# A two-layer recurrent block: unlooped projections, turned logits behind the next queries, three queues for a group's loads, wider gate rows

## What is computed

```python
x = L0_attn_x                                    # 2 x 2048 x 256, float32
xn = _layernorm(x)
s = _L0_attn_ref(xn, ...)                        # 16 heads of width 16, full attention, plus xn
g = _silu(_L0_ffn_ref(xn, ...))                  # 8 experts, two branches, gelu router, cumulative sums
x = x + s * g
xn = _layernorm(x)
s = _L1_attn_ref(xn, ...)                        # 16 heads, band |i - j| <= 64
g = _silu(_L1_ffn_ref(xn, ...))                  # below
x = x + s * g

def _L1_ffn_ref(x, weight, gate_w, lora_U, lora_V):
    gate = softmax(xt @ gate_w.T)                # 8 experts
    base = xt @ weight.T
    t = einsum('nh,erh->ner', xt, lora_U)        # 8 x 16 values per token
    lora = einsum('ne,eor,ner->no', gate, lora_V, t)
    return base + lora / 16
```

## Time and profile before

| | us |
|---|---|
| median of 3 runs | 2477.73 |
| lowest, highest | 2476.5, 2492.4 |
| profiled execution | 2464.94 |
| its span | 2463.20 |
| PE busy | 2211.5 (90% of the span) |
| DVE busy | 1840.1 (75%) |
| ScalarE busy | 1448.6 (59%) |
| POOL busy | 463.5 (19%) |
| mean granted PE clock | 0.952 |

### The profile page before, as it was taken

One profiled execution on the slowest core, in us unless ns is written; L12 is line 12 of the kernel. 1 busy time (PEld: TensorE's weight loads), 2 busy tenths in 40 slices (PEclk: granted clock), 3 DMA queues, 4 the chain that ended last, 5 costly groups with the idle time before them and its releaser, 6 DMA issues. The chain is left out here.

```text
span 2463.2 us, 44369 instructions
## 1 busy us (share of the span) xinstructions
PE 2211.5 (90%) x14912; PEld 1233.5 (50%) x14912; DVE 1840.1 (75%) x3240; ACT 1448.6 (59%) x2165; POOL 463.5 (19%) x673
## 2 busy tenths in 40 slices
PE   7786799999999999999999999988999986799988
PEld 5564333333333333333333333326888875566688
DVE  5553999999999999999999999913443565788846
ACT  4443177777777777777777777771222222266743
POOL 0000000000000000000000000003455510266745
PEclk8998599999999999999999999999999988589999
DMA  6766700310500500402205002006567469666564
GB/s 212 260 238 196 93 4 6 47 22 5 61 5 8 61 3 12 57 6 36 31 5 61 7 8 61 3 5 188 155 172 177 103 235 355 130 134 154 153 166 129
DMA packets 189121, 231.80 MB, mean 94 GB/s; under 512 B 72720, under 2 KB 122768, under 8 KB 186064
## 3 DMA queue, kind: packets, MB, share of 16 engines
q1 hardware_dynamic: 176048, 210.46, 35.0%
q10 hardware_dynamic: 7184, 14.10, 2.8%
q0 software_dynamic: 5728, 5.00, 0.9%
HBM read 138.97 MB, written 89.13 MB: 93 GB/s over the span
## 5 line engine op out<-in xcount | busy, mean ns | idle before, releaser
L1015 DVE TENSOR_REDUCE a_maxes<-a_ps_a 128x2 f32<-128x1024 f32 x1024 | 1202.3, 1221 | 112.0 <-PE a_ps_a L1136 108.3
L1080 ACT ACTIVATE a_prob<-a_ps_s 128x512 f32<-128x512 f32 (+1 forms) x1376 | 1035.8, 804 | 347.5 <-PE a_ps_s L1162 341.5
L1162 PE MATMUL a_ps_s<-a_Q,a_K 50*128 50x512 f32 x2048 | 593.8, 452 | 90.7 <-ACT a_prob L1080 90.4
L1136 PE MATMUL a_ps_a<-a_K,a_Q 48*128 48x512 f32 x2048 | 549.9, 454 | 25.6 <-DMA a_Q<-s_halves 14.2
L1174 PE MATMUL a_ps_o<-a_prob,a_V 128*17 128x512 f32 x4096 | 539.8, 599 | 0.1
L1162 PEld LDWEIGHTS a_ps_s<-a_Q,a_K 50*128 50x128 f32 x2048 | 277.4, 185 | 505.8 <-ACT a_prob L1080 456.6
L1136 PEld LDWEIGHTS a_ps_a<-a_K,a_Q 48*128 48x128 f32 x2048 | 244.9, 189 | 229.7 <-issue 107.9
L973 POOL DMA_DIRECT2D a_Q<-a_m_parts x128 | 64.5, 504 | 1285.3 <-DVE a_m_parts L1007 1278.6
L1626 ACT ACTIVATE a_prob<-a_ps_s 128x512 f32<-128x512 f32 (+1 forms) x256 | 135.7, 583 | 111.6 <-PE a_ps_s L1717 110.5
L1566 DVE CUSTOM_DVE_ANT_0 a_scratch<-a_ps_a,k_mask 128x256 f32<-128x256 f32 (+1 forms) x512 | 177.9, 411 | 30.0 <-PE a_ps_a L1681 28.0
L1681 PE MATMUL a_ps_a<-k_K,k_Q 48*128 48x256 f32 (+1 forms) x512 | 122.2, 363 | 32.5 <-PEq L89 21.7
(11 more groups left out here) (186 smaller groups left out, 2225.3 us busy)
## 6 DMA issues: line engine op xcount, KB each, us to landing
s_halves<-p_parts SPq DMA_DIRECT2D x64, 512.0 KB, 5.3
s_xT<-p_xT SPq DMA_DIRECT2D x64, 256.0 KB, 4.4
a_Q<-s_halves SPq DMA_DIRECT2D x186, 64.0 KB, 10.4
a_K<-s_halves SPq DMA_DIRECT2D x42, 256.0 KB, 9.6
s_v<-p_v_out SPq DMA_DIRECT2D x16, 544.0 KB, 4.5
s_cT<-p_cT SPq DMA_DIRECT2D x32, 256.0 KB, 3.6
k_wb<-s_w SPq DMA_DIRECT2D x16, 512.0 KB, 7.6
c_wb<-s_w SPq DMA_DIRECT2D x16, 512.0 KB, 7.2
```

What stands on the lines that cost most here:

```text
L1015: nc.vector.tensor_reduce(maxes[:, :, slot, qt, kc], ps_a[:, o:o + 2 * CH].rearrange("p (z k) -> p z k", z=2), AX.X, ALU.max).then_inc(a_d ...
L1080: nc.scalar.activation(prob[:, ring:ring + len(t), :].rearrange("p r q -> p (r q)"), ps_s[:, bank:bank + len(t) * CH], ACT.Exp, scale=scal ...
L1136: last = nc.tensor.matmul(ps_a[:, o + side * CH:o + (side + 1) * CH], Q[rows, q0:q0 + P], K[rows, k0:k0 + CH], start=True, stop=True)
L1162: last = nc.tensor.matmul(ps_s[:, bank + x * CH:bank + (x + 1) * CH], K[rows, k0:k0 + P], Q[rows, q0:q0 + CH], start=True, stop=True)
```

## The change

There are three parts.

1. `phase_project`: the three pairs of the loop are written out on all five engines, in both layers. In layer 0 the transposes of a chunk's logits (`turn_logits`) stand behind the next chunk's `queries_keys` on PE, and DVE's `logits` behind the next chunk's `rests(i, u, (2, 3))`. The last chunk's stand at the end.
2. Band: of the second group's loads SP keeps the keys of side 0 and has them ahead of `store_maxima(0)`; ScalarE keeps the keys of side 1, ahead of the ones; POOL gets all queries, under a semaphore of its own, for which PE waits too.
3. Last stage: `front` is one product with 392 columns (gate, U and weight together) into c_ps_x (4 banks), the attention projection goes to c_ps_s (2 banks), and c_ps_m keeps 2. `front`, `maximum` and `softmax` run three tiles ahead instead of two. `maximum` and `softmax` stand at the end of their engine's work for a tile. The wait of `front` on `wt_done` is gone; that on `out_read` stays, with OUTS = 4, and now stands ahead of the whole product.

The diff, cut to its core:

```diff
@@ -517,7 +517,7 @@
                         second_halves(sp, 0)
                     store_values(sp, i, u)
 
-            with sp.Fori(0, NCH - 1) as i:
+            for i in range(NCH - 1):
                 chunk_pair(i, True)
...
                     rests(i, u, (2, 3))
+                    if first and 2 * i + u > 0:
+                        logits(*divmod(2 * i + u - 1, 2))
...
                         row_statistics(nc, dve, L, i + 1, u, passed)
-                    if first:
-                        logits(i, u)
...
                 chunk_pair(i, True)
             chunk_pair(NCH - 1, False)
+            if first:
+                logits(NCH - 1, 1)
...
                 last.then_inc(log_ready, 1)
+
+            def turn_logits(c):
                 wait_apart(pe, logT_done, 2 * (c + 1), passed)
...
             def chunk_pair(i, more):
                 for u in range(2):
                     queries_keys(i, u)
+                    if first and 2 * i + u > 0:
+                        turn_logits(2 * i + u - 1)
                     if u == 0:
...
                 chunk_pair(i, True)
             chunk_pair(NCH - 1, False)
+            if first:
+                turn_logits(2 * NCH - 1)
...
-def load_next(eng, S, KQ, side, g, k):
-
-    done = KQ["loaded"][g % BAND_BUFS]
+def load_next(eng, S, KQ, side, g, k, done=None):
+
+    done = done or KQ["loaded"][g % BAND_BUFS]
...
-            return LOADS * (g // BUFS + 1) - (LOADS - EARLY_LOADS if g % BUFS == 0 else 0)
+            return LOADS * (g // BUFS + 1) - (LOADS - EARLY_LOADS, 2 * PARTS, 0)[g % BUFS]
...
+            for k in range(0, PARTS, 2):
+                load_next(sp, S, KQ, 0, 1, k)
             store_maxima(0)
-            for k in range(PARTS):
-                load_next(sp, S, KQ, 0, 1, k)
             load_v(sp, 0)
             load_v(sp, 1)
...
+            for k in range(1, PARTS, 2):
+                for side in range(2):
+                    load_next(pool, S, KQ, side, 1, k, pool_loaded)
             for s in range(STEPS):
                 mask(s)
...
+            for k in range(0, PARTS, 2):
+                load_next(act, S, KQ, 1, 1, k)
             for side in range(2):
                 for row in range(2):
                     r = side * SIDE + ROW_M0 + row
                     act.dma_start(f32(K[r:r + 1, :]), W["ones"][:, 0:BUFS * LONG // P]).then_inc(rows_set, DMA)
-            for k in range(PARTS):
-                load_next(act, S, KQ, 1, 1, k)
...
                         pe.wait_ge(kq_loaded[g % BUFS], loads_of(g) * DMA)
+                    if g == 1:
+                        pe.wait_ge(pool_loaded, 2 * PARTS * DMA)
...
         OUTS = 4
-        ps_gt = n_.ps("ps_gt", 2 * CH)
-        ps_out = n_.ps("ps_out", OUTS * CH)
+        ps_x = n_.ps("ps_x", OUTS * CH)
+        ps_s = n_.ps("ps_s", 2 * CH)
         ps_m = n_.ps("ps_m", 2 * CH)
...
             def front(i, j):
                 u, t = order[j]
                 n = TILES_BODY * i + j
-                gt, g = (j % 2) * CH, (j % OUTS) * CH
+                o = (j % OUTS) * CH
                 c = 2 * i + u
...
                 x = lambda s, k: xT[c % BUFS][:, s, k, t * P:(t + 1) * P]
-                pe.wait_ge(wt_done, n + 1)
-                split_matmul(nc, ps_gt[:, gt:gt + NGT], x, lambda s, k: W["gate"][:, s, k, 0:NGT], DK,
-                             True, True).then_inc(gt_ready, 1)
                 pe.wait_ge(out_read, n + 1)
-                split_matmul(nc, ps_out[:, g:g + D], x, lambda s, k: W["gate"][:, s, k, NGT:], DK,
-                             True, False)
+                split_matmul(nc, ps_x[:, o:o + NGT + D], x, lambda s, k: W["gate"][:, s, k, :], DK,
+                             True, False).then_inc(gt_ready, 1)
...
             def out(i, j):
                 n = TILES_BODY * i + j
-                g = (j % OUTS) * CH
+                g, o = (j % OUTS) * CH + NGT, (j % 2) * CH
+                pe.wait_ge(out_read, OUTS + n - 1)
                 pe.wait_ge(high, n + 1)
                 pe.wait_ge(low, 2 + n + 1)
 
-                split_matmul(nc, ps_out[:, g + D:g + 2 * D], lambda s, k: turned[:, j % 2, s, k * P:(k + 1) * P],
-                             lambda s, k: W["o1"][:, s, k, :], DK, False, True)
-                split_matmul(nc, ps_out[:, g:g + D], lambda s, k: turned[:, j % 2, s, D:D + P],
+                split_matmul(nc, ps_s[:, o:o + D], lambda s, k: turned[:, j % 2, s, k * P:(k + 1) * P],
+                             lambda s, k: W["o1"][:, s, k, :], DK, True, True)
+                split_matmul(nc, ps_x[:, g:g + D], lambda s, k: turned[:, j % 2, s, D:D + P],
                              lambda s, k: W["loraV"][:, s, 0, :], 1, False, True).then_inc(out_ready, 1)
...
             def body(i, more):
                 for j in range(TILES_BODY):
-                    if ahead(i, j, 2, more):
-                        front(*ahead(i, j, 2, more))
+                    if ahead(i, j, 3, more):
+                        front(*ahead(i, j, 3, more))
                     if ahead(i, j, 1, more):
                         turn(*ahead(i, j, 1, more))
                     out(i, j)
 
             front(0, 0)
             front(0, 1)
+            front(0, 2)
...
+                gt = (j % OUTS) * CH
+                act.wait_ge(top_done, n + 1)
+                if n > 1:
+                    act.wait_ge(soft, 2 * (n - 1))
+                nc.scalar.activation(ge[:, j % 2], ps_x[:, gt:gt + E1], ACT.Exp, bias=neg_top[:, j % 2:j % 2 + 1],
+                                     accum_out=total[:, j % 2:j % 2 + 1]).then_inc(ge_done, 1)
...
             def body(i, more):
                 for j in range(TILES_BODY):
-                    if ahead(i, j, 2, more):
-                        softmax(*ahead(i, j, 2, more))
                     if ahead(i, j, 1, more):
                         copies(*ahead(i, j, 1, more))
                     exponential(i, j)
+                    if ahead(i, j, 3, more):
+                        softmax(*ahead(i, j, 3, more))
...
+                gt = (j % OUTS) * CH
                 dve.wait_ge(gt_ready, n + 1)
-                nc.vector.tensor_reduce(neg_top[:], ps_gt[:, gt:gt + E1], AX.X, ALU.max, negate=True
-                                        ).then_inc(soft, 1)
+                if n > 1:
+                    dve.wait_ge(ge_done, n - 1)
+                nc.vector.tensor_reduce(neg_top[:, j % 2:j % 2 + 1], ps_x[:, gt:gt + E1], AX.X, ALU.max, negate=True
+                                        ).then_inc(top_done, 1)
...
             def body(i, more):
                 for j in range(TILES_BODY):
-                    two, one = ahead(i, j, 2, more), ahead(i, j, 1, more)
-                    if two:
-                        maximum(*two)
+                    three, two, one = (ahead(i, j, k, more) for k in (3, 2, 1))
                     if one:
                         rest(*one)
                     if two:
                         gates(*two)
-                    n, slot, g = TILES_BODY * i + j, j % 2, (j % OUTS) * CH
+                    n, slot, g = TILES_BODY * i + j, j % 2, (j % OUTS) * CH + NGT
                     gate_steps(nc, dve, n, sums[:, slot], W["bo"][:, 1], (x1_done, n + 1),
-                               gate[:, slot], eg[:, slot], ps_out[:, g + D:g + 2 * D],
-                               ps_out[:, g:g + D], exp_done, step, out_read, x1_done)
+                               gate[:, slot], eg[:, slot], ps_s[:, slot * CH:slot * CH + D],
+                               ps_x[:, g:g + D], exp_done, step, out_read, x1_done)
+                    if three:
+                        maximum(*three)
```

More of the change, by code:

```diff
@@ L532, in _ @@
         def _(pool):
-            with pool.Fori(0, NCH - 1) as i:
+            for i in range(NCH - 1):
                 for u in range(2):
@@ L617, in _ @@
             transposed(0, 0)
-            with dve.Fori(0, NCH - 1) as i:
+            for i in range(NCH - 1):
                 chunk_pair(i, True)
             chunk_pair(NCH - 1, False)
+            if first:
+                logits(NCH - 1, 1)
         @block.scalar
@@ L677, in _ @@
             turned(0, 0)
-            with act.Fori(0, NCH - 1) as i:
+            for i in range(NCH - 1):
                 chunk_pair(i, True)
@@ L755, in _ @@
             transposes(0, 0)
-            with pe.Fori(0, NCH - 1) as i:
+            for i in range(NCH - 1):
                 chunk_pair(i, True)
             chunk_pair(NCH - 1, False)
+            if first:
+                turn_logits(2 * NCH - 1)
 NG2 = NG // B
@@ L2155, in phase_combine_lora @@
         att = n_.sb("att", [P, BUFS, TT, D])
[L2156 to L2158 removed]
+        neg_top = n_.sb("neg_top", [P, 2])
+        ge = n_.sb("ge", [P, 2, E1])
+        total = n_.sb("total", [P, 2])
         inv = n_.sb("inv", [P, 1])
@@ L2291, in softmax @@
                 n = TILES_BODY * i + j
-                gt = (j % 2) * CH
-                act.wait_ge(soft, 3 * n + 1)
```

(8 more changed lines are left out.)

22 lines of the change are left out of this document (11 added, 11 removed).

## The result

| | us |
|---|---|
| before, median of 20 runs | 2476.39 |
| changed, median of 20 runs | 2492.31 |
| ratio, 95% interval | 1.0062, 1.0046 to 1.0078 |
| changed, profiled execution | 2485.8 (span 2484.2) |

The changed kernel is slower by 0.62%, some 15 us; the forecast was +11.1 (0.45%).

The account below looks back on a forecast made before the run. TensorE was taken to bound layer 0's projection, band and last stage, DMA layer 1's projection. Terms -22 + 0 - 5.5 + 38.6 = +11.1 on the 2477.73 median gave 2489 us; own range 2474 to 2502, 8 in 10 2466 to 2540.

Parts of the forecast that it names:

- Last stage, +38.6: Last stage: PE waits for DVE's gate before 28 fronts, tile 4.16 against 2.78 us, +38.6; bounds +33 to +45.
- The handoff: Last stage: 0.1 us from the gate's end at T + 2.77 to PE's six merged rows.
- the bound of 4.0 a tile: Last stage's lower bound: a tile period of 4.0 us with handoffs hidden, giving +33.
- Layer 0, -22: Layer 0's projection: moved logits -11.1, written-out loops -5.8 and clock -5, in sum -22; bounds -15 and -23.
- The logits' term of 11.1: Layer 0: seven of eight waits of 1.58 us before the turned logits go, -11.1.
- table loads and clock together (5.8 and 5): Layer 0, loops written out: five activation table loads go, -5.8; half-speed rows after their gaps go, -5 of 6.2.
- Layer 1, 0: Layer 1's projection: DMA engines are full, so gains wait at the stores of s_halves; 0, bounds -2 and +1.
- Band, -5.5: Band's start: second group's loads land at 2122.3, shortening PE's 8.04 us wait by 5.5; bounds 0 and 8.0.
- The clock did not fall in the last stage: First rival, last stage: pauses lower PE's clock, tile some 6.0 us, total 2540, or 2514 for half; chance 0.25.
- The second, that the wait does not bite: Second rival, last stage: DVE frees the banks before PE arrives; -37 in all, 2441; chance 0.07.
- If nothing else happened: Last stage: merged rows cost 0.30 us less than 1.37 per tile, so 32 tiles would give -9.6.
- The third rival: Projection and band: only moved logits pay, -11, and the band 0; total +28, 2505; chance 0.08.

Follow-up runs that it names:

- front behind out: The changed kernel with PE issuing front(j+3) after out(j) instead of ahead of turn(j+1): 2448.14 us, ratio 0.9875 to the kernel before.
- one gate step: front behind out, plus ScalarE's copies ahead of softmax (two tiles ahead) and c_weight dropped, its factor in the LoRA V weights: 2433.64 us, 0.9816 of before.

## Why the prediction was right

**Last stage, +38.6; measured +40.6 and +42.1.** This was the term that decides, and its mechanism held to the hundredth where it rests on rows of before: the gate ended at T + 2.77. Two small numbers were off. The handoff was 0.05, not 0.1. The six rows took 1.19 from start to start (2416.02 to 2417.21), not 1.07; without a wait ahead of them they take 1.07 (2392.36 to 2393.43 with front behind out) to 1.08 (2376.81 to 2377.89 with one gate step). So they cost 0.11 more after a pause, which unbroken rows can't show: in the stream the weight load of the first starts 0.11 ahead of its matmul (2376.70), behind the wait the two start together (2416.02). Tile 4.23 against 4.16. The 1.07 itself was partly luck: between 0.75 for 256 columns and 1.39 for 512 (1942.39 to 1943.78) interpolation gives 1.09, and 1.07 is 392/512 of 1.40. And the bound of 4.0 a tile gives +34, not +33. On the price of the rows the estimate by the Trainium skill, "TensorE: Matmul & The Clock Gate", section "Wait — 56ns, not 53.3ns?", was 0.995 for six; the traces have 1.07 to 1.08 in the stream.

**Layer 0, -22; measured -20.7, and -20.3 in the means.** The logits' term of 11.1 was measured as 12.8, table loads and clock together (5.8 and 5) as 7.1. The clock's share was put down to the table loads alone; that step was wrong. Of the four slow stretches that it counted in the kernel before, the two of h went with the table loads, and the two of queries stand behind the logits' wait. With the loops alone written out two stretches of slow queries were left, about 3 us, which is most of what is missing from the 10.8.

**Layer 1, 0; measured +1.6** over thirteen profiles, a little above my upper bound of 1. That whatever the engines gain waits at the stores fits what was measured, since the stage's own work kept its length; what the term lacks is the idle time between the last values and the band, 1.8 longer in the mean, and its cause stays open.

**Band, -5.5; measured -6.1 at the wait and -6.0 in the stage's mean.** The whole 8.04 went, and 1.9 came back at the maxima, which the prediction had named. But the 5.5 was worked out differently, as 8.04 less a wait of 2.55 for the queries; these landed at about 2105.4, 0.8 behind 2104.64, where PE came to stand, and the maxima at 2106.56 hid that. So the size is right in part by luck. POOL was faster at the issue than forecast, 6.1 us for twelve and not 10. By the Trainium skill, "DMA: Bandwidth & Descriptors", section "Issuing engines are not separate DMA queues", several issuers save only the time of the issue, which the prediction put at 3.4. The gain is more, since SP's loads had stood behind the wait for the maxima too, and not only behind the issue of their stores. The DMA engines were not full all that time: a window of the kernel before, which stands between the two at 1.06 and 0.94, has a share of 0.41:

```profile
2111.00:2117.00 6.00, 6.00 (x20) 4.48 (x19) 6.00 (x36) 0.00 (x0) 0.00 (x0) 0.50 0.41 51
```

In the changed kernel the share is 0.78 from 2082 to 2088 and 1.02 to 1.09 from 2088 to 2106.

**The rivals.** The clock did not fall in the last stage (1.00 there), with pauses of 1.50 in every 4.2 us. The second, that the wait does not bite, fell with the first tile, but its price, -9.6 for merged rows, was wrong too: with the wait out of the way the stage gained 0.7 and 1.2. The step that failed there is "If nothing else happened": the tile before was bound twice, by PE (2.78) and by the ring over DVE and ScalarE (2.76 to 2.78), and I read only the first. The third rival, -11 in layer 0 and nothing in the band, fell with -20.3 and -6.0.

The sum of what was measured, -20.3 - 6.0 + 1.6 + 40.6, is +15.9, and the medians differ by 15.9. That they agree to the tenth is luck, as one stage alone varies by several us from profile to profile. The forecast of +11.1 missed by 4.8: 2.0 in the last stage, 1.7 in layer 0 and 1.6 in layer 1, less 0.5 in the band. The lower end of my own range, 2474, doesn't follow from the bounds: their lowest values add up to 0, which is 2478.

## What to carry to other kernels

When buffers are merged or work is put further ahead, count for each wait which tile it now names, and then where in the engine's queue it stands: the same wait cost 41 us ahead of 1.4 us of ready work and nothing behind it. Before a faster engine is priced, look for a second ring of nearly the same length; here PE's 2.78 and a ring of 2.76 to 2.78 over the other engines lay on each other, and a gain on one alone was worth nothing. A wait can be worth more than its length, by what the clock does behind it: in layer 0 seven waits of 1.58, 11.1 in all, were worth 12.8. In the last stage 28 waits of 1.5 were not, and that part can't be counted from one profile.

## What the runs showed of the hardware

- A DVE instruction of 8 columns between SBUF tiles took 0.65 us beside a POOL addition and 0.23 without, while a DVE instruction that reads PSUM (rest) kept its 0.56 beside one, and a reciprocal of one column its 0.15.
- Six matmuls of 392 columns cost 1.07 to 1.08 from start to start in an unbroken stream and 1.19 behind a pause of 1.50.
- The same band took 253 to 265 us from one profile to the next, at a granted clock of 0.88 to 0.82 (nine profiles); in the kernel before, windows of 6 us from 2130 to 2148 show 0.50 although PE was busy 5.93 to 6.00 of each.
- A loop's body kept its table loads in each round, three at each of two places; written out, one of six stayed.
- A pause of 1.50 in every 4.2 us did not lower the clock in the last stage; in layer 0, with waits of 1.55 and 1.57 in each chunk of 21 us, it fell in two of the seven later chunks.
